# A recurrence feeding a mixture of experts on one core: scaling and copying the first pair's gates on VectorE in place of ScalarE

## The reference, cut to what matters

```python
# x: 32 rows x 32 steps x 128 features, h0: 32 x 128; E=16 experts, K=4 chosen
xw = einsum('ntd,dh->nth', x, Wx) + b
h_t = tanh(xw_t + h_{t-1} @ Wh)                      # 32 steps, one after another
xn = h * rsqrt(mean(h*h, -1) + 1e-5) * norm_scale
logits = xn @ wg + bg
vals, idx = top_k(logits, 4); gates = softmax(vals)  # per token
gate_full = gates laid out over the 16 experts, 0 elsewhere
for each expert e:
    g = xn @ w1[e] + b1[e]
    a = minimum(g[::2], 7); l = clip(g[1::2], -7, 7)
    s = a * sigmoid(1.702 * a) * (l + 1)
    y_e = s @ w2[e] + b2[e]
out = x + h + sum_e gate_full[:, e] * y_e            # 1024 tokens x 128
```

## Time and profile before

| what | value |
|---|---|
| median of three runs | 103.24 us |
| the profiled execution's own time | 102.98 us |
| its span (first to last instruction) | 100.9 us |
| outside the span, 102.98 - 100.9 | 2.08 us |
| PE busy | 95.8 us, 95% |
| DVE busy | 73.0 us, 72% |
| ACT busy | 69.5 us, 69% |
| POOL busy | 73.1 us, 73% |
| granted TensorE clock | 1.00 in every stretch |

### The profile page before, as it was taken

How to read it: one execution, slowest core, us unless ns; L and a number is a source line. 1 busy time by engine, 2 the same in 40 slices (tenths; PEclk the granted TensorE clock), 3 DMA queues, 4 the chain that set the end, 5 groups by cost and what they waited for, 6 DMA issues and landing times.

```text
span 100.9 us, 1849 instructions
## 1 busy us (share of the span) xinstructions
PE 95.8 (95%) x589; PEld 82.0 (81%) x590; DVE 73.0 (72%) x187; ACT 69.5 (69%) x158; POOL 73.1 (73%) x83
## 2 busy tenths in 40 slices
PE   6999999999999999999999899999999999999970
PEld 2666678799999899999999688888878888889750
DVE  0306699689599785995879987669796977969630
ACT  3335997989685956769388668668887898996000
POOL 6001239993769993499817999999999999899400
PEclk9999999999999999999999999999999999999999
DMA  2998960017920009950499004992100000000012
GB/s 53 237 328 282 408 236 0 6 47 302 375 120 0 6 7 226 387 223 7 133 340 351 15 4 121 305 365 95 48 7 0 6 0 0 0 0 0 6 52 52
DMA packets 5001, 12.99 MB, mean 129 GB/s; under 512 B 752, under 2 KB 1792, under 8 KB 4992
## 3 DMA queue, kind: packets, MB, share of 16 engines
q1 hardware_dynamic: 4672, 12.66, 36.4%
q10 hardware_dynamic: 320, 0.21, 0.8%
HBM read 12.28 MB, written 0.59 MB: 128 GB/s over the span
## 4 chain that ended last, share of the span: by engine, by line
PE 31%; POOL 30%; DVE 11%; issue 10%; DMA 7%; ACT 4%; POOLq 2%; SPq 2%; DVEq 0%
POOL actg L461 15%; POOL act_lo L470 10%; PE psA L913 8%; DMA w_sb<-in_w 7%; PE psB L913 7%; PE psY L957 5%; POOL w_lo L477 3%; DVE lin L792 2%; POOLq L86 2%; PE psM L969 2%; PE psY L858 2%; PE psR L858 2%; PE psY L969 2%; PE psM L874 1%; DVE act L810 1%
## 5 line engine op out<-in xcount | busy, mean ns | idle before, releaser
L792 DVE TENSOR_SCALAR lin<-psB,one_b1b 128x256 f32<-128x256 f32 (+1 forms) x48 | 25.9, 568 | 11.2 <-PE psB L913 10.9
L586 ACT ACTIVATE psA<-psA,lim_b1a 128x256 f32<-128x256 f32 (+1 forms) x48 | 23.9, 515 | 11.6 <-PE psA L913 11.6
L461 POOL TENSOR_TENSOR actg<-act,gate_cols 128x512 f32<-128x512 f32 x25 | 31.9, 1289 | 0.0
L598 ACT ACTIVATE psA<-psA,limit_col 128x512 f32<-128x512 f32 x32 | 21.1, 659 | 0.8
L810 DVE SCALAR_TENSOR_TENSOR act<-lin,psA 128x512 f32<-128x512 f32 x26 | 17.8, 686 | 1.7 <-ACT psA L598 0.6
L913 PE MATMUL psA<-xn_hi,w_hi 128*128 128x256 f32 (+1 forms) x48 | 18.0, 376 | 0.4 <-DVE act L810 0.3
L913 PE MATMUL psB<-xn_hi,w_hi 128*128 128x256 f32 (+1 forms) x48 | 15.8, 330 | 0.0
L470 POOL TENSOR_TENSOR act_lo<-actg,act_hi 128x512 fp32r<-128x512 f32 x12 | 15.4, 1300 | 0.4 <-ACT act_hi L550 0.4
L913 PE MATMUL psB<-xn_lo,w_hi 128*128 128x256 f32 (+1 forms) x48 | 15.3, 318 | 0.0
L913 PE MATMUL psB<-xn_hi,w_lo 128*128 128x256 f32 (+1 forms) x48 | 15.3, 318 | 0.0
L913 PE MATMUL psA<-xn_hi,w_lo 128*128 128x256 f32 (+1 forms) x48 | 15.3, 319 | 0.0
(11 more groups left out here) (112 smaller groups left out, 190.4 us busy)
## 6 DMA issues: line engine op xcount, KB each, us to landing
gate_cols<-gate_rows SPq DMA_DIRECT2D x16, 512.0 KB, 5.5
w_sb<-in_w SPq DMA_DIRECT2D x4, 512.0 KB, 7.5
w_sb<-in_w SPq DMA_DIRECT2D x4, 256.0 KB, 8.6
out<-yT SPq DMA_DIRECT2D x3, 128.0 KB, 1.7
wx_x_sb<-in_wx_x SPq DMA_DIRECT2D x1, 320.0 KB, 4.7
wx_x_sb<-in_wx_x SPq DMA_DIRECT2D x2, 128.0 KB, 2.6
small_h<-in_small ACTq DMA_DIRECT2D x1, 105.0 KB, 2.7
gate_rows<-gT SPq DMA_DIRECT2D x4, 16.0 KB, 1.5
```

What stands on the lines that cost most here:

```text
L461: nc.gpsimd.tensor_tensor(by_pair(actg[:, u % SUM_DEPTH, w]), by_pair(act[:, u % ACT_DEPTH, w]), gate_block(u, w), ALU.mult).then_inc(actg ...
L586: last = nc.scalar.activation(psA[u % 2][:, o], psA[u % 2][:, o], ACT.Relu, scale=-1.0, bias=lim_b1a[:, e0 + k:e0 + k + 1])
L598: nc.scalar.activation(psA[u % 2][:, 0:w], psA[u % 2][:, 0:w], ACT.Gelu_apprx_sigmoid, scale=-1.0, bias=limit_col[:, :]).then_inc(swish_do ...
L792: last = nc.vector.tensor_scalar(lin[:, v % 2, o], psB[v % 2][:, o], one_b1b[:, e0 + k:e0 + k + 1], LIMIT + 1.0, ALU.add, ALU.min)
```

## The change

In ScalarE's list the two scaling instructions of pair 0 and the copy of pair 0 are gone. Pairs 1 to 3 are as before. VectorE gets two functions. `scale_first` does the same scaling by two `tensor_scalar` instructions with the inverse as a per-partition scalar, behind `act` of unit 0. `copy_first` copies the 16 rows of psX to `gT`, between `lin` and `act` of unit 1, and waits for the transposes.

```diff
@@ ScalarE, loop over the units
                 for t in steps_at(u, 1):
                     tanh(t)
-                if u == GATES[0]:
-                    scale_gates(0)
                 for q in at(GATES_T, u):
-                    copy_gates(q)
+                    if q:
+                        copy_gates(q)
@@ VectorE
+            def scale_first():
+
+                dve.wait_ge(inv_ready, 1)
+                for j in pair_tiles(0):
+                    last = nc.vector.tensor_scalar(
+                        gates_w[:, j, :].rearrange("p (a b e) -> p a b e", a=3, b=2)[:, :, 0, :],
+                        gate_sum[:, j, :].rearrange("p (a e) -> p a e", a=1).to_broadcast([P, 3, E]),
+                        inv[:, j:j + 1], None, ALU.mult)
+                last.then_inc(scale_done, 1)
+
+            def copy_first():
+
+                dve.wait_ge(gates_mm, 1)
+                nc.vector.tensor_copy(gT[:, 0:PW], psX[0:E, 0:PW]).then_inc(gT_ready, 1)
@@ VectorE, loop over the units
                 for q in at(GATES, v):
                     close_gates(q)
+                if v == GATES_T[0]:
+                    copy_first()
                 if v < NU:
                     ... lin_done, swish_done, act of unit v
+                if v == GATES[0]:
+                    scale_first()
```

## The result

The changed kernel is slower: a median of 104.18 us (22 runs) against 103.34 us for the kernel before (22 runs), ratio 1.0068 with a 95% interval of 1.0049 to 1.0088, so 0.5 to 0.9 us lost. The forecast was 0.21 us gained, the range 102.65 to 103.85. Medians here are over all runs and ratios over undisturbed ones, which are 14 and 18 of the 22, with medians of 103.82 and 103.30 us. The one median lies above the range and the other at its upper edge, and both moved the other way than the forecast.

A forecast was written before the change was run, and what follows sets the result against it. The bound was taken as the wait chain over ScalarE's first-pair gate scalings to TensorE's step at 23.45. s = 17.89 plus 5.35 put that step 0.21 us earlier, so 103.24 - 0.21 = 103.03 us, range 102.65 to 103.85.

The forecast's parts named there:

- the price of the scalings: Pair 0's two scalings on VectorE: 0.27 us for one, 0.17 between starts, the first starting at 17.45.
- s: End of the first pair's gate scaling: 17.52 before, forecast 17.89 after, 0.37 us later.
- rival 1: VectorE's scalings lose the SBUF port to GpSimd: +0.52 us with one wait (chance 0.26), +1.33 with two (0.06).
- the product at 93.5: VectorE's 256-column product near the kernel's end: 1.12 us, its twin 0.41, ending 0.28 after GpSimd's product.
- The lock: Skill's rule: SBUF's second port pair is held exclusively by GpSimd or VectorE for a whole instruction.
- The law from s to step 16: From the scaling's end to TensorE's step at 23.45: s + 5.35, giving 23.24, or 0.21 us earlier.
- step 16: TensorE's recurrence step loaded at 23.45 before the change, ahead of unit 4's b half; forecast about 23.25.
- Carried to the end: What the loop's first units gain or lose was taken to reach the kernel's end whole.
- Rival 3: Later chain pieces hide the 0.2 us gain, so nothing is carried on: 103.24 us, chance 0.04.
- The copy: Copy to gT on VectorE between lin and act of unit 1: 0.41 us, its wait for the transposes holding nothing.

The follow-up runs named there:

- e4: The changed kernel with GpSimd waiting for the end of VectorE's scalings before its low parts of w1; ratio 0.9954 to the kernel before.
- e5: The changed kernel with GpSimd's ten low parts of w1 of 256 columns made as five of 512; ratio 1.0428 to the kernel before.
- e9: The changed kernel with one harmless 128-column copy from PSUM on VectorE ahead of the two scalings; ratio 1.0075 to the kernel before.
- e6: The changed kernel with one tensor_tensor, both inputs in SBUF, in place of the two scalings; ratio 0.9950 to the kernel before.
- e10: The changed kernel with a harmless PSUM copy ahead of one SBUF tensor_tensor that replaces the two scalings; ratio 0.9938 to the kernel before.
- e3: The changed kernel with the first pair's gate sums in PSUM, where the two scalings read them; ratio 0.9947 to the kernel before.
- e7: The changed kernel with the first pair's gate sums in PSUM and the two scalings ahead of act of unit 0; ratio 0.9922 to the kernel before.
- e8: The changed kernel with gate sums in PSUM and one tensor_tensor for both scalings, ahead of act of unit 0; ratio 0.9881 to the kernel before.
- e15: The same kernel as e8, run again for a tighter interval and another trace; ratio 0.9921 to the kernel before.
- e2: The kernel before with only the copy to gT moved to VectorE, scalings left on ScalarE; ratio 0.9982 to the kernel before.
- e1: The kernel before with only the two scalings moved to VectorE, copy to gT left on ScalarE; ratio 1.0082 to the kernel before.

## Why the prediction was wrong

- **The step that failed** is the price of the scalings: "0.27 for one and 0.17 to 0.19 between starts", so s = 17.89. Measured on the clock of the earlier trace rows it was 19.19 - 0.26 = 18.93, with 0.80 and 0.76 us each. I had taken L758, which ran at 3.50, when GpSimd was idle. So the sum put the wait for GpSimd at nothing and left it to a rival. The right price was that of rival 1, with 0.26 of the chances for one wait and 0.06 for the two that happened.
- **My size of rival 1** was 1.33 us for two waits; the trace has 0.93. I let an instruction end 0.28 behind GpSimd's, from the product at 93.5, and added a whole instruction behind each end. The scalings ended 0.05 and 0.04 behind, and the second waited only for the very next GpSimd instruction, which had begun at 18.43, before the first scaling ended.
- **The lock** decided this time. The Trainium skill (SBUF — State Buffer, SBUF: two separate sides) has the pair locked for a whole instruction. e4, e5 and e9 agree: 0.24 us with GpSimd idle, 1.2 to 1.3 beside its 1.27 us, ends tied to its seams. Its rule that whoever starts first gets the pair agrees with e6 and e10. The changed kernel's scaling was recorded 0.03 ahead of GpSimd's and still lost, which the recorded starts neither explain nor hold against the rule, as said at e10.
- **The law from s to step 16 held.** s + 5.35 is, behind the inverse, the transposes' load plus 5.30. That gives 7.53, 7.36, 6.91, 6.48 and 6.44 for the changed kernel, e9, e10, e3 and e4; measured 7.59, 7.41, 6.98, 6.54 and 6.50. It holds where the scalings stand behind `act` and the clock stays at 1.00, so not for e5, e7, e8 and e15.
- **Carried to the end:** right. 0.90 at step 16 became 0.93 at the end, 0.15 in e3 became 0.12. Rival 3 falls. Of e4's 0.19, 0.11 arrived.
- **The copy** cost nothing that shows, as argued (0.03 at the end in e2).
- **Missed:** 0.3 us less outside the span, which no row of the trace shows. With it the trace's 0.93 is about 0.6, beside a measured 0.5 to 0.9; and e3, 0.12 in the trace, is 0.3 to 0.8 faster in time.

## What to carry to other kernels

Before work goes to VectorE, look at what GpSimd does at that moment. A `tensor_scalar` of 0.25 us that reads and writes SBUF cost 0.8 beside a GpSimd run, and a source in PSUM took it out of the contest. Not every instruction is held: the last section has some that were not. An engine freed ahead of a wait gains nothing if what it waits for comes later by the same edit: follow the moved result to its first reader.

## What the runs showed of the hardware

TensorE's clock in e5, by windows (length, busy us and counts of PE, PEld, DVE, ACT and POOL, then the granted clock):

```profile
17.00:20.00 3.00, 1.50 (x11) 1.08 (x9) 2.96 (x7) 2.01 (x6) 3.00 (x3) 1.00 0.00 0
20.00:22.00 2.00, 1.22 (x6) 1.20 (x7) 2.00 (x5) 0.29 (x1) 2.00 (x3) 0.72 0.04 8
22.00:24.00 2.00, 2.00 (x12) 2.00 (x11) 0.43 (x1) 0.87 (x3) 1.74 (x2) 0.50 0.04 8
24.00:26.00 2.00, 2.00 (x18) 2.00 (x18) 1.29 (x3) 1.47 (x5) 0.00 (x0) 0.93 0.37 127
```

TensorE's matmuls had stood still 2.25 us for the scalings. Behind that the granted clock was 0.50, the 1.2 GHz level, and a matmul of the a half took 0.41 us instead of 0.28. This is what e5 lost beyond the two longer waits: 6.76 us from the transposes to step 16, where the changed kernel and e1, e3, e4, e6, e9 and e10 have 5.35 to 5.37. In the changed kernel the matmuls stood still 1.31 us and the clock was 1.00 in the same stretches. What a wait between these two lengths would have done, no run shows.

Some instructions of the kernel before were not held. VectorE's reduces and reciprocal, with one input in SBUF, run under GpSimd's low parts of w1. A subtraction of 512 columns with two inputs in SBUF runs under GpSimd's exponent:

```profile
16.09 6.94 POOL L444 TENSOR_TENSOR w_lo<-w_sb,w_hi 128x256 fp32r<-128x256 f32 x10
...
16.38 0.28 DVE L709 TENSOR_REDUCE gate_sum<-hot 128x32 f32<-128x128 f32 x1
16.57 0.15 DVE L710 TENSOR_REDUCE den<-expo 128x2 f32<-128x8 f32 x1
16.76 0.17 DVE L714 RECIPROCAL inv<-den 128x2 f32<-128x2 f32 x1
```

```profile
8.72 0.69 DVE L746 TENSOR_TENSOR w_lo<-w_sb,w_hi 128x512 fp32r<-128x512 f32 x1
...
14.32 1.33 POOL L422 TENSOR_TENSOR expo<-euler,diff 128x6 f32<-128x6 f32 x1 [1.80 <-DVE diff L687]
...
14.99 0.69 DVE L746 TENSOR_TENSOR w_lo<-w_sb,w_hi 128x512 fp32r<-128x512 f32 x1
```

The reduces and the reciprocal took 0.28, 0.15 and 0.17 us, against GpSimd's 0.72 for one instruction. The subtraction took 0.69 us from 14.99, beside GpSimd's exponent of 14.32 to 15.65 (a rough span, as the profile's are for GpSimd), and it took 0.69 at 8.72 too, with GpSimd idle. So neither a source in SBUF on VectorE nor a running GpSimd instruction is enough for a wait. What sets these apart from the scalings, no run here tests.
